# Two counting sorts of a graph network on one core: one table per group by wide matmuls, all scatter indices kept, the scatters written out

## The reference

```
x = _layernorm(x + _L0_gnn_ref(x, edge_attr_3, edge_weight1, ..., edge_index), axis=-1)   # segments by row = src
x = _layernorm(x + _L1_gnn_ref(x, ..., src, dst), axis=-1)                                # segments by dst
x = _layernorm(x + _L2_gnn_ref(x, edge_index, edge_attr_16, ...), axis=-1)
x = _layernorm(x + _L3_gnn_ref(x, edge_index, edge_weight, ...), axis=-1)
...
agg = jax.ops.segment_sum(m, dst, num_segments=h.shape[0])
```

## Time and profile before

| | us |
|---|---|
| median of 3 runs | 10206.86 |
| lowest, highest | 10171.75, 10210.83 |
| span of the profiled execution | 12340.5 |

### The profile page before, as it was taken

The page is one execution under the profiler, slowest core; times in us unless marked ns, Lnnn a source line. Parts: engine busy times, 40 slices in busy tenths (PEclk is TensorE's granted clock), DMA queues, the critical chain, the costliest instruction groups (busy, mean ns, idle before and its releaser), DMA issues. The chain is left out here.

```text
span 12340.5 us, 143767 instructions
## 1 busy us (share of the span) xinstructions
PE 5470.3 (44%) x34831; PEld 4903.5 (40%) x34831; DVE 5430.0 (44%) x13782; ACT 1621.9 (13%) x3916; POOL 6695.6 (54%) x6579
## 2 busy tenths in 40 slices
PE   5555545666555444443333364333365222232223
PEld 4444435666534444443333353333344222222223
DVE  6444433333377444443554575333356333333334
ACT  0111111111144111111000053000044000000000
POOL 2555534555443555554666553665554666646664
PEclk7555557777777555556655586555577555665556
DMA  0000005555433000002444343333343111111111
GB/s 6 1 1 1 1 24 152 165 162 158 141 97 97 1 1 1 1 1 88 131 130 130 116 135 83 82 84 83 83 122 112 43 44 43 44 48 44 44 44 41
DMA packets 872078, 859.23 MB, mean 70 GB/s; under 512 B 310368, under 2 KB 703464, under 8 KB 871654
## 3 DMA queue, kind: packets, MB, share of 16 engines
q0 software_dynamic: 211680, 350.82, 10.5%
q1 hardware_dynamic: 279328, 391.67, 9.8%
q10 hardware_dynamic: 381024, 116.23, 3.8%
HBM read 651.02 MB, written 207.06 MB: 70 GB/s over the span
## 5 line engine op out<-in xcount | busy, mean ns | idle before, releaser
L984 PE MATMUL sum_ps_sum<-sum_hot,sum_msg 128*128 128x128 f32 x8820 | 1432.0, 326 | 2009.5 <-issue 1598.9
L984 PEld LDWEIGHTS sum_ps_sum<-sum_hot,sum_msg 128*128 128x128 f32 x8820 | 1303.2, 233 | 2216.7 <-issue 1778.6
L765 PE MATMUL scores_ps_x<-scores_win,scores_hot_t 128*128 128x128 f32 (+1 forms) x5292 | 1069.2, 362 | 1277.7 <-DVE scores_act_m L820 569.5
L765 PEld LDWEIGHTS scores_ps_x<-scores_win,scores_hot_t 128*128 128x128 f32 x5292 | 1024.5, 296 | 1338.2 <-DVE scores_act_m L820 582.0
L947 DVE TENSOR_TENSOR acc<-acc,sum_ps_sum 128x128 f32 x2520 | 726.8, 288 | 1611.0 <-remote 1030.4
L418 POOL DMA_INDIRECT payload_dst<-load_dst_pay_slot,load_dst_at_i x882 | 850.3, 964 | 929.2 <-issue 755.9
L418 POOL DMA_INDIRECT payload_src<-load_src_pay_slot,load_src_at_i x882 | 870.8, 987 | 890.2 <-issue 731.0
L721 POOL DMA_INDIRECT scores_rows<-kv_table,scores_idx x882 | 833.8, 945 | 758.7 <-issue 302.2
L721 POOL DMA_INDIRECT scores_rows<-h_table,scores_idx x882 | 839.1, 951 | 715.3 <-issue 286.6
L721 POOL DMA_INDIRECT scores_rows<-xl_table,scores_idx x882 | 886.8, 1005 | 549.2 <-issue 264.0
L917 POOL DMA_INDIRECT sum_rows<-x_table,sum_idx x882 | 871.4, 988 | 561.3 <-ACT sum_idx L908 292.0
(11 more groups left out here) (388 smaller groups left out, 12064.7 us busy)
## 6 DMA issues: line engine op xcount, KB each, us to landing
spill<-scores_rows SPq DMA_DIRECT2D x378, 448.0 KB
sum_rows<-spill SPq DMA_DIRECT2D x378, 448.0 KB
scores_win<-q_table ACTq DMA_DIRECT2D x882, 64.0 KB
scores_win<-xr_table ACTq DMA_DIRECT2D x882, 64.0 KB
payload_src<-load_src_pay_slot,load_src_at_i POOLq DMA_INDIRECT x882
scores_rows<-kv_table,scores_idx POOLq DMA_INDIRECT x882
payload_dst<-load_dst_pay_slot,load_dst_at_i POOLq DMA_INDIRECT x882
scores_rows<-xl_table,scores_idx POOLq DMA_INDIRECT x882
```

What stands on the lines that cost most here:

```text
L765: mm = pe.matmul(ps_x[:, j, 0:window_w], hot_t[:, s, j, :], win[:, s, j, :], start=True, stop=True)
L984: mm = pe.matmul(ps_sum[:, s, j, :], msg[:, s, j, :], hot[:, s, j, :], start=True, stop=True)
```

## The change

The change rewrites the second block of both sorts, and nothing else computes differently.

- `ps_lo` and its matmul (L324) are gone, as is DVE's compare for `one_lo_t` (L381). PE transposes the one-hot tables instead (seven transposes a group into `ps_lo_t`), and ACT copies them to `lo_t` in SBUF.
- The running table `ps_run`, its 882 copies on ACT and the chain between ACT and PE are gone. For tile j of a group PE multiplies the tile's one-hot tables once with the `hi` table broadcast over all later tiles, 350, 300, ... 50 columns wide, into one PSUM table `ps_tab`. One DVE addition of 128x400 elements puts the base of the group under all eight tables (`tab`); its last 50 columns are the next group's base.
- One-hot tables have three slots (`lo3`, `hi3`), table and `lo_t` live in scratch memory of `acc`.
- `at_i` holds all 882 columns, and POOL scatters straight from `pay`. The slots, ACT's payload copies and SP's part in the loop are gone. POOL waits once per group for `at_ready`, and its 882 DMAs are written out without a loop. The loops of PE and DVE handle six groups a turn in place of two.

```diff
+                def tables(g, s):
+                    pe.wait_ge(ranked, G * g + G)
                     for j in range(G):
...
+                        col = bass.ds(g * G + j, 1)
+                        pe.matmul(ps_key[:, j, :], lo_bf[:, col].to_broadcast([P, P]), c.ident_bf[:], start=True, stop=False)
+                        mm = pe.matmul(ps_key[:, j, :], hi_bf[:, col].to_broadcast([P, P]), c.ident_bf[:],
+                                       start=False, stop=True)
+                    mm.then_inc(keys_spread, 1)
+                    pe.wait_ge(compared, n_cmp * (g + 1))
+                    pe.wait_ge(lo_t_ready, g + 1)
                     for j in range(G):
-                        k = (s * G + j) % 2
-                        pe.wait_ge(snapped, gi * G + (j + 1))
-                        pe.matmul(ps_run[:, 0:HB], one_lo[:, s, :, j], one_hi[:, s, :, j], start=False, stop=True,
-                                  skip_group_check=True).then_inc(ran, 1)
-                        if count_next is not None:
-                            if j == 0:
-                                pe.wait_ge(next_ready, 2 * gi + 2)
-                            pe.matmul(ps_counts[:, 0:HB], next_one_lo[:, s, :, j], next_one_hi[:, s, :, j], start=False,
-                                      stop=True, skip_group_check=True)
-                        pe.matmul(ps_look[:, j, 0:HB], one_lo_t[:, s, j, :], running[:, k, :],
-                                  start=True, stop=True).then_inc(looked, 1)
+                        mm = pe.transpose(ps_lo_t[:, j, :], lo3[:, s % SB3, :, j], c.ident_bf[:])
+                    mm.then_inc(lo_turned, 1)
+                    pe.wait_ge(tabled, g + 1)
+                    for j in range(G):
+                        later = ps_tab[:, s % PS2, (j + 1) * HB:(G + 1) * HB].rearrange("p (n h) -> p n h", h=HB)
+                        mm = pe.matmul(later, lo3[:, s % SB3, :, j],
+                                       hi3[:, s % SB3, :, j].rearrange("p (o h) -> p o h", o=1).to_broadcast([P, G - j, HB]),
+                                       start=(j == 0), stop=True, skip_group_check=True)
+                    if count_next is not None:
+                        for j in range(G):
+                            mm = pe.matmul(ps_counts[:, 0:HB], next_lo3[:, s % SB3, :, j], next_hi3[:, s % SB3, :, j],
+                                           start=False, stop=True, skip_group_check=True)
+                    mm.then_inc(tallied, 1)
+
+                def look_up(g, s):
+                    pe.wait_ge(lo_t_ready, g + 2)
+                    pe.wait_ge(tabled, g + 3)
+                    pe.wait_ge(picked_read, g + 1)
+                    for j in range(G):
+                        mm = pe.matmul(ps_look[:, j, 0:HB], lo_t[:, s % PS2, j, :], tab[:, s % SB3, j, :],
+                                       start=True, stop=True)
+                    mm.then_inc(looked, 1)
...
+                pe.sem_inc(tallied, 3)
+                pe.sem_inc(looked, 3)
+                pe.wait_ge(zeroed, 2)
+                tables(0, 0)
+                with pe.Fori(0, R // 6 - 1) as i:
+                    for s in range(6):
+                        tables(6 * i + s + 1, s + 1)
+                        look_up(6 * i + s, s)
...
+                def turned(g, s):
+                    act.wait_ge(lo_turned, g + 1)
+                    act.wait_ge(looked, g + 2)
+                    act.copy(lo_t[:, s % PS2], ps_lo_t[:, 0:G, :]).then_inc(lo_t_ready, 1)
...
-                    dve.wait_ge(spread, gi + 1)
-                    dve.tensor_scalar(one_lo_t[:, s], ps_lo[:, 0:G, :], c.lane[:, 0:1], None,
-                                      ALU.is_equal).then_inc(lo_t_ready, 1)
+                        dve.tensor_tensor(next_lo3[:, s], column_g[:], per_tile(group(next_lo, g), P),
+                                          ALU.is_equal).then_inc(compared, 1)
...
+                def rank_and_add(g, s):
+                    dve.wait_ge(keys_spread, g + 1)
                     for j in range(G):
...
+                        dve.scalar_tensor_tensor(same[:, j, :], ps_key[:, j, :], pay[:, bass.ds(g * G + j, 1), 0],
                                                  c.before[:], ALU.is_equal, ALU.mult,
-                                                 accum_out=rank[:, s, j:j + 1]).then_inc(ranked, 1)
-                    dve.wait_ge(ranked, gi * G + G)
-                    dve.sem_inc(keys_read, 1)
...
+                                                 accum_out=rank[:, s % SB3, j:j + 1]).then_inc(ranked, 1)
+                    dve.wait_ge(tallied, g + 4)
+                    dve.wait_ge(looked, g + 1)
+                    dve.wait_ge(tabled, g + 2)
+                    base = tab[:, (s + 2) % SB3, G, :]
+                    dve.tensor_tensor(tab[:, s % SB3], ps_tab[:, s % PS2, 0:(G + 1) * HB].rearrange("p (n h) -> p n h", h=HB),
+                                      per_tile(base, G + 1), ALU.add).then_inc(tabled, 1)
+
+                def place(g, s):
+                    dve.wait_ge(looked, g + 4)
+                    dve.tensor_tensor(picked[:], hi3[:, s % SB3].rearrange("p h g -> p g h"), ps_look[:, :, 0:HB],
+                                      ALU.mult).then_inc(picked_read, 1)
+                    dve.wait_ge(picked_read, g + 2)
+                    dve.tensor_reduce(at[:], picked[:], AX.X, ALU.add).then_inc(at_summed, 1)
+                    dve.wait_ge(at_summed, g + 1)
+                    dve.wait_ge(ranked, G * g + 2 * G)
+                    dve.tensor_tensor(group(at_i, g), at[:], rank[:, s % SB3], ALU.add).then_inc(at_ready, 1)
+                    dve.wait_ge(at_ready, g + 1)
...
+                with dve.Fori(0, R // 6 - 1) as i:
+                    for s in range(6):
+                        compare(6 * i + s + 2, s + 2)
+                        rank_and_add(6 * i + s + 1, s + 1)
+                        place(6 * i + s, s)
...
-                with pool.Fori(0, R // 2) as i:
-                    for s in range(2):
-                        gi = 2 * i + s
-                        pool.wait_ge(staged, gi + 1)
-                        pool.wait_ge(at_ready, gi + 1)
-                        pool.sem_inc(pool_go, 1)
-                        for j in range(G):
-                            pool.indirect_dma_start(
-                                o.payload, bass.IndirectOffsetOnAxis(ap=at_i[:, s, j:j + 1].bitcast(U32), axis=0),
-                                pay_slot[:, s, j, :], None).then_inc(scattered[s], 16)
+                for t in range(T):
+                    if t % G == 0:
+                        pool.wait_ge(at_ready, t // G + 1)
+                    pool.indirect_dma_start(
+                        o.payload, bass.IndirectOffsetOnAxis(ap=at_i[:, t:t + 1].bitcast(U32), axis=0),
+                        pay[:, t, :], None).then_inc(scattered, 16)
...
-                sp.sem_inc(slot_free, 2)
-                with sp.Fori(0, R // 2) as i:
-                    for s in range(2):
-                        sp.wait_ge(scattered[s], 16 * G * (i + 1))
-                        sp.sem_inc(slot_free, 1)
+                sp.wait_ge(scattered, 16 * T)
```

131 lines of the change are left out of this document (56 added, 75 removed).

## The result

The kernel after the change took 10227.6 us (median of 20 runs, 10222.4 to 10238.5), and the kernel before, in the same session, 10211.45 (20 runs, 10171.75 to 10218.51). The ratio is 1.0018, 95% interval 1.0012 to 1.0025. So the change made the kernel slower, by 16 us between the medians or 18 by the ratio, and I had forecast 41 us the other way.

What follows compares the result with a forecast made beforehand. The prediction took POOL issuing indirect DMAs to bound the kernel, in sorts and gathers. Its terms, -44 for slots and +3 for the start, gave -41 against 10206.9, so 10166 us, with an eight-in-ten range of 9950 to 10290.

Steps and rivals of the forecast that it cites:

- the term of -44 us for the slots: POOL in the sorts: waits for a slot go, 0.65 us in place of 0.30 over 126 groups; 44 us saved.
- It keeps up, with 0.8 us to spare: Old sort loop: the slot's circle takes 8.03 us while POOL is busy 8.84 with the other slot.
- The sum that backed the term: Median less 2308.8 leaves seven stages 7898 us, about 109 above POOL's own rate; the sorts' share is 48.
- I take it for an effect of recording: Sorts: POOL's 8.54 us idle after fourteen DMAs, with DVE and ACT held on PE's results, was blamed on the profiler.
- Start: Before POOL's first DMA of a sort: DVE takes 11.0 us in place of 9.6; +3 us for both sorts.
- they can't pass 1.6 ns a column: PE's seven wide matmuls, 1400 columns a group: at most 2.24 us, at least 1.20, taken as 1.7.
- the prediction's sum for PE: PE's work a group at the low clock: 7.8 to 8.8 us in src, 7.2 to 8.3 in dst, under 8.84.
- The look-ups: PE's look-ups, two passes each with weight loads taking 0.53 us: 3.71 us a group.
- B: Rival: the two slots do cost in real runs; most of it 9850 to 10110 us, chance 0.25.
- C: Rival: PE becomes the bound and the kernel slower; 10660 us at twice the upper bound, chance 0.10.
- D: Rival: 882 written-out DMAs or long loop bodies cost by themselves; 0.1 us a DMA gives 10345, chance 0.03.
- If POOL's pitch stays and the time falls by hundreds, my reading of the stall is wrong: Sign against taking the sorts' stall in the trace for an effect of recording.

Runs made afterwards that it cites:

- With POOL silent: Changed kernel with six semaphores, POOL starting its scatters only when all indices are there, against the kernel before: 11760.32 us (quick).
- the added matmuls: Changed kernel with every transpose of L326 on PE issued three times, against the kernel before: 12262.83 us, ratio 0.9851 (held).
- the two kernels meant to settle it: Changed kernel with six semaphores: POOL scattering after all indices (1.1543), or a memset ahead of each scatter (1.0136), against the kernel before, quick.

## Why the prediction was wrong

**The step that failed is the term of -44 us for the slots**, that is 126 times the one gap of 0.65 us in place of 0.30. In the quick trace of before POOL has 0.30 behind every scatter but 14. There was nothing to save at the slots: the full index table without a gap (six semaphores, 0.9987) stands no better than the new tables on two slots with their gaps (0.9985). The right reading was in the prediction already, "It keeps up, with 0.8 us to spare": the slot's circle did not bind, and the saving should have stood at zero. The trace could have warned me too: of its 125 slot changes in the src sort 11 have 0.6 to 0.7 us, 50 have the usual 0.30, and the others have longer holds.

**The sum that backed the term** was right in size and wrong in meaning. It subtracted 2308.8 us of a held trace from a median of the quick condition, two conditions side by side. That it came out near is because the rest of the kernel hardly differs between them, which I had not checked: the quick trace gives 96 us above POOL's own rate for the seven stages where I had 109, and 48 for the two sorts, where I had 48. But these 48 us are no waits for slots. They are 19 us of gaps at each 112th scatter and 30 us of long scatters, and the change, which leaves both kinds of cost in place, raised them to 37 and 44.

**"I take it for an effect of recording"** was wrong as to the cause. The profiler holds nothing: in the quick condition the profiled execution is as long as the runs (span 10179.5, runs 10184.8), and in the held one the runs are as slow as the profile (12109 to 12131, profiled span 12122.5). That the stall was not in the times then compared was right, by the luck that they were all of the quick condition.

**What was missing** are two costs. The gaps, 1.69 us at every 112th scatter before, became 2.95 us at every 113th, 18 us for both sorts; six semaphores took them away, in the trace and in the time. The compares beside scatters added some 15 us by the traces, for which no time of its own was found. Signs of both could be seen ahead of the change. The earlier trace rows has scatters of up to 1426 and 1477 ns in the sorts and none over 977 in the first gather. And the held trace of before has the gaps beside its pauses, seven a sort at the same places, of 1.69 or 2.22 us. Behind the 113th scatter of the dst sort:

```profile
4220.32 0.96 POOL L418 DMA_INDIRECT payload_dst<-load_dst_pay_slot,load_dst_at_i  x1 [2.22 <-issue]
```

That one semaphore on all scatters would lengthen them, no row of before could tell.

**Part by part.** POOL: scatters still 0.96 and 1.263 apart, as costed. Start: first scatter 1.0 us later by the traces (166.9 and 165.9), in place of 3 for both. DVE's L401 took 0.57 us, below the 0.7 to 0.95 expected; ACT's copy 0.91, under its bound. PE's seven wide matmuls stood at the upper end of their range, and the first and the last line here are a group's look-ups:

```profile
308.26 3.17 PE L345 MATMUL load_src_ps_look<-acc 128*128 128x50 f32 x14
312.72 0.95 PE L326 MATMUL load_src_ps_lo_t<-const_ident_bf,load_src_lo 128*128 128x128 bf16 x7
313.47 2.38 PE L331 MATMUL load_src_ps_tab<-load_src_hi,load_src_lo 128*128 128x350 bf16 x7
315.67 0.77 PE L336 MATMUL load_src_ps_counts<-load_src_next_hi,load_src_next_lo 128*128 128x50 bf16 x7
316.26 1.71 PE L345 MATMUL load_src_ps_look<-acc 128*128 128x50 f32 x14
```

The 2.38 us run to the end of the last one. From the first start to that of the next kind, as the prediction's rows are read, it is 2.20 us, within 1.2 to 2.24 and above the 1.7 taken. So by the row "they can't pass 1.6 ns a column" held, with 1.57. The rule of the Trainium skill on 16-byte lines (Advanced Engine Details and Errata, section SBUF Cachelines), by which they would stand at or above the upper bound, was a better guide than the middle, though they came out just under that bound. The granted clock did not matter to these matmuls: the median group of seven took 2.38 us at a granted 0.5 and 2.36 at 1.0, where the transposes went from 0.95 to 0.57 and the look-ups from 3.17 to 1.71.

That clock is what the prediction's sum for PE, 7.8 to 8.8 us a group in src, left out. It was made for the low level, and there it was right: the 11 groups of the src sort that ran wholly at a granted 0.5 took 8.0 us in the median. But the granted clock of that sort rose from 0.55 to 0.68 with the change, in the quick traces, and the 13 groups wholly at 1.0 took 5.9. With POOL silent PE and DVE made a group in some 7.0 us (125 groups in the 877), at a granted 0.72, PE busy all but 3 of the 877. The look-ups were over-sized, 3.71 us a group by a row of two weight loads in 0.53, against 3.17 at the low level. Over both levels their group in the profile after (busy, mean ns of one, idle before) gives 295.7 us for 125 groups, 2.4 each:

```profile
L345 PE MATMUL load_src_ps_look<-acc 128*128 128x50 f32 x1750 | 295.7, 337 | 0.9 <-DVE load_src_picked L406 0.9
```

**The rivals.** B, slots that cost in real runs, gives the size seen in the held condition: the gain there is 2.5%, within the time span I gave to it. Its cause is not shown. In the changed kernel, which has no slots, it is PE that holds the sort; how much of the gain is from the slots and how much from the chain between ACT and PE was not run, for the new tables with two slots never met that condition. In the condition of the result B was worth nothing. C, PE as the bound: rejected in the quick condition, 7.0 under 8.84, and POOL waited for indices less than 1 us beyond its start. D: rejected, at least for POOL's code. My sign "If POOL's pitch stays and the time falls by hundreds, my reading of the stall is wrong" came true in the held sessions, by 315 us.

**Open.** What makes PE crawl some 11 us into a stretch of dense scatters. Its weight loads and matmuls then wait for "issue" only, which would fit a late supply of instructions, but this is argued; the added matmuls fell between the theories, and the two kernels meant to settle it never met the held condition. Also open is what the gap at each 84th to 113th scatter is:

| kernel | semaphores | slots | quick | held |
|---|---|---|---|---|
| before | 2 | 2 | 1.69 us each 112 | 1.69 or 2.22 each 112 |
| before, six semaphores | 6 | 2 | not run | 1.57 each 84, some shorter |
| changed | 1 | none | 2.95 each 113 | 2.95 each 113 |
| changed, two semaphores | 2 | none | not run | none |
| changed, six semaphores | 6 | none | none | none |
| changed tables, ring of two | 2 | 2 | 1.69 each 112 | not run |
| changed tables, ring of six | 6 | 6 | none | 1.57 each 84 |

Neither the number of semaphores nor that of slots decides alone.

## What to carry to other kernels

Before anything is summed, put the span of the profile beside the median of the runs. If they differ by a fifth, as here, the two may be from two conditions, and the profile has to be taken again in the one that is timed. A sum across both can come out near, as mine did, and still not say what the excess consists of: that needs the trace of the condition that is timed. Where indirect DMAs back to back are the bound, look at the gap behind each one by its number (a gap each hundred hides in any median), and try their increments on more than one semaphore: that paid with the full index table (1.0018 to 0.9987, quick), but not on the two slots of before (1.0055, held). Look also at what a scatter meets: VectorE compares with both inputs in SBUF lengthened some, though what that costs in time was not found. A cost read from a row holds for that row's granted clock. No version was the best in both conditions: the ring of six slots in the quick one (0.9954, but 0.9777), the full index table in the held one (0.974, but 0.9987 with six semaphores and 1.0018 with one).

## What was not expected of the hardware

The same program took 10185 us and, on the same chip in a later session, 12440. With a single semaphore on 882 indirect DMAs POOL idled 2.95 us behind every 113th. A DVE compare with two SBUF inputs lengthened a scatter from 0.96 to as much as 1.55 us. A memset of 0.22 us on GpSimd between two indirect DMAs cost 0.09 of pitch, the rest fitting into the 0.30 that is idle between them anyway. Seven wide matmuls that read every seventh element took 2.38 us at a granted clock of 0.5 and 2.36 at 1.0.
